# A four-layer residual stack with an RNN and an LSTM: tanh arguments in PSUM, and the LSTM's output product on GpSimd

## The chip, the cores and the metric

The kernel runs on one core of a Trainium2 chip. The metric is the device time of one execution in microseconds. The kernel before takes 3935.61 us (median of 3 runs, 3935.6 to 3937.57).

## The reference

The input x has 4 sequences of 1024 tokens of 512 numbers. Four layers follow one another, each added to its input:

```python
x = x + rnn(x)      # h = tanh(x_t @ Wx + b + h @ Wh), 1024 steps
x = x + ssm(x)      # convolution, projections, a decaying state, output projection
x = x + lstm(x)     # A = x_t @ Wx + b + h @ Wh
                    # i, f, o = sigmoid(A parts), g = tanh(A part)
                    # c = f * c + i * g ;  h = o * tanh(c), 1024 steps
x = x + x @ layer   # a layer made from the condition, once per sequence
```

The RNN and the LSTM each start from a given 4 x 512 state and are sequential: a step needs the h of the step before. The LSTM's Wh is 512 x 2048, the RNN's 512 x 512.

## The kernel before

**Chunks.** The tokens are cut into 32 chunks of 32 steps. The layers are staggered: while the RNN works on chunk i, the state-space layer works on chunk i - 1, the LSTM on chunk i - 2 and the output layer on chunk i - 3 (`chunk_work`). Each engine runs its own `body` for a chunk; the first and last chunks are written out, the others run in a loop of two chunks (`pipeline`). In a full chunk every one of the 32 steps holds one LSTM step, one RNN step and a slice of the other layers' work. There are 1024 LSTM steps; the two first chunks have RNN steps alone (64 of them).

**An LSTM step.** The state h is kept as two fp16 parts, a rounded value and the rest (`hls`), because the products with Wh, itself in two parts, are made in fp16. TensorE makes them in two halves of 256 columns (half 0 and half 1, each with its own PSUM bank `psL0`, `psL1`; 32 matmuls each, L1024 to L1046). It needs the h of half 0 first, and after 24 matmuls the h of half 1. For each half the following comes in turn; the halves are interleaved on VectorE by an order written out by hand (L866 to L890), and VectorE executes it strictly in that order:

- VectorE transposes the sums out of PSUM into `tr` (L745) and reduces them with the input part, which GpSimd had copied there (`fill`, L351), to the gates' arguments `arg` (L750).
- ScalarE makes all four gates with one tanh (`gates`, L487; sigmoid is made from tanh of half the argument), and the output gate's scaled copy `o_s` (L492).
- VectorE makes the two products i*g and f*c in one instruction (`products`, L756) and the cell (`new_cell`, L761). The cell lies beside the gates in one tile, so that one instruction can read both.
- ScalarE makes the cell's tanh (`tanh_cell`, L496).
- VectorE makes h in fp32 (`h_part`, L778, read again by the subtraction and by the next layer's input), h rounded to fp16 (`hi_part`, L781) and their difference as fp16 (`lo_part`, L785). The last one tells TensorE.

The RNN step is alike and simpler: transpose L854, reduction L859 to `arg_r`, tanh L510, the fp16 parts L898 and L900. It lies in the same queues: its transpose between the cell of half 0 and the products of half 1, its reduction ahead of `lo_part` of half 1, its fp16 parts at the end of the step, after whatever the state-space layer does on VectorE (`ssm_stage`).

**GpSimd.** In each step it copies the LSTM's input for step s + 2 into `tr`, one copy a half, each when the reduction of that half of step s is over; then the RNN's input (`fill_rnn`, L365). Every fourth step it adds the RNN's or the LSTM's outputs to the residual (L370, L377; sums of two tensors, 128 x 64).

**PSUM.** `psL0`, `psL1` and `psR` are banks of 512 fp32 columns. The matmuls of the LSTM use 256 columns of the first two, those of the RNN 128 of the third.

## Time and profile before

| | |
|---|---|
| median of 3 runs | 3935.61 us |
| lowest and highest | 3935.6 and 3937.57 us |
| span of the profiled execution | 3932.7 us |
| busy, share of the span | TensorE 92%, its weight load 78%, VectorE 83%, ScalarE 44%, GpSimd 20% |
| granted TensorE clock, mean | 0.995 of full |

The profiled execution's own total time is not among the numbers shown; what stands beside its span is the median, 2.9 us above it. The profile gives for each engine the busy time, the groups of instructions that cost most, who waited for whom, a timeline, and the chain of work that ended last. "Busy" of VectorE and ScalarE is from an instruction's start to its acknowledged end; the next one can start a little before that end, so lengths of instructions that stand one behind the other add up to more than the time they take together. Idle time is counted only from the end of the last instruction.

### The profile page before, as it was taken

The numbers are of one execution on the slowest core, as the hardware profiler recorded it, in microseconds if no ns is written. First come the engines' busy times: TensorE is split into PE (matmuls) and PEld (weight loads), VectorE is DVE, ScalarE is ACT, GpSimd is POOL, SyncE is SP. The second block draws the span as 40 slices with busy tenths as digits, with TensorE's granted clock in tenths as the row PEclk, the third lists the DMA queues.
The fourth block names the chain that finished last, engine by engine and source line by source line (L and its number), as shares of the span: only waits on it lengthen the run. The fifth ranks groups of instructions, "written<-read, shape, count | busy, mean of one in ns | idle before, by whom it ended". The sixth has DMA issues, their size and how long they took to land.

```text
span 3932.7 us, 255334 instructions
## 1 busy us (share of the span) xinstructions
PE 3630.1 (92%) x110596; PEld 3058.0 (78%) x110596; DVE 3273.3 (83%) x19155; ACT 1748.5 (44%) x8244; POOL 774.4 (20%) x3623
## 2 busy tenths in 40 slices
PE   7899999999999999999999999999999999999875
PEld 4688788888888788888888888888888888877654
DVE  6588888888888888888888888888888888888766
ACT  4244444444444444444444444444444444444432
POOL 0122222222222222222222222222222222212111
PEclk9899999999999999999999999999999999999999
DMA  7100000000000000000000000000000000000000
GB/s 275 48 7 7 10 10 10 7 7 10 10 10 9 9 7 7 10 10 10 10 7 7 10 10 10 10 7 10 7 10 10 10 10 7 7 7 7 7 6 8
DMA packets 19109, 63.32 MB, mean 16 GB/s; under 512 B 3958, under 2 KB 4526, under 8 KB 14914
## 3 DMA queue, kind: packets, MB, share of 16 engines
q1 hardware_dynamic: 17692, 46.67, 3.7%
q8 instruction: 868, 14.22, 1.5%
q14 instruction: 255, 2.09, 0.2%
q10 hardware_dynamic: 294, 0.33, 0.0%
HBM read 38.48 MB, written 8.39 MB: 12 GB/s over the span
## 4 chain that ended last, share of the span: by engine, by line
DVE 55%; PE 39%; issue 4%; ACT 1%; SPq 1%; DMA 0%; ACTq 0%; DVEq 0%; POOL 0%; POOLq 0%
PE ps_lstm L1027 32%; DVE lstm_sums L745 19%; DVE lstm_arg L750 8%; DVE lstm_ig_fc L756 7%; DVE lstm_gates_2c L761 5%; DVE rnn_sums L854 5%; DVE lstm_h_parts L785 3%; DVE lstm_h_scaled L778 2%; DVE lstm_h_parts L781 2%; PE ps_rnn L1066 2%; PE ps_lstm_in_b L1108 1%; PE ps_lstm_in_a L1171 1%; PE ps_ssm L1108 1%; SPq L301 1%; DVE rnn_h_parts L900 1%
## 5 line engine op out<-in xcount | busy, mean ns | idle before, releaser
L1027 PE MATMUL ps_lstm<-lstm_Wh_parts,lstm_h_parts 128*20 128x256 f16 x65472 | 1973.3, 273 | 259.4 <-DVE lstm_h_parts L785 246.8
L1027 PEld LDWEIGHTS ps_lstm<-lstm_Wh_parts,lstm_h_parts 128*20 128x20 f16 x65472 | 1543.1, 91 | 665.2 <-DVE lstm_h_parts L785 509.9
L487 ACT ACTIVATE lstm_gates_2c<-lstm_arg 128x32 f32<-128x32 f32 x2048 | 469.8, 229 | 1354.7 <-DVE lstm_arg L750 1354.7
L745 DVE STREAM_TRANSPOSE lstm_sums<-ps_lstm 128x256 f32<-128x256 f32 x2048 | 912.2, 445 | 191.5 <-PE ps_lstm L1027 157.4
L351 POOL COPY lstm_sums<-lstm_in 128x32 f32<-128x32 f32 x2048 | 423.7, 210 | 1749.8 <-DVE lstm_arg L750 1749.8
L1066 PE MATMUL ps_rnn<-rnn_Wh_parts,rnn_h_parts 128*20 128x128 f16 x32736 | 638.8, 220 | 22.4 <-DVE rnn_h_parts L900 20.3
L1066 PEld LDWEIGHTS ps_rnn<-rnn_Wh_parts,rnn_h_parts 128*20 128x20 f16 x32736 | 549.5, 92 | 56.2 <-DVE rnn_h_parts L900 38.5
L750 DVE TENSOR_REDUCE lstm_arg<-lstm_sums 128x32 f32<-128x96 f32 x2048 | 537.9, 263 | 35.2
L496 ACT ACTIVATE lstm_tanh_c<-lstm_gates_2c 128x8 f32<-128x8 f32 x2048 | 410.4, 200 | 253.7 <-DVE lstm_gates_2c L761 253.7
L510 ACT ACTIVATE rnn_h<-rnn_arg 128x16 f32<-128x16 f32 x1024 | 220.9, 216 | 515.8 <-DVE rnn_arg L859 515.7
L492 ACT ACTIVATE lstm_o_scaled<-lstm_gates_2c 128x8 f32<-128x8 f32 x2048 | 428.0, 209 | 33.4
L781 DVE TENSOR_TENSOR lstm_h_parts<-lstm_o_scaled,lstm_tanh_c 128x8 f16<-128x8 f32 x2048 | 332.6, 162 | 130.4 <-ACT lstm_tanh_c L496 79.1
L756 DVE SCALAR_TENSOR_TENSOR lstm_ig_fc<-lstm_gates_2c 128x16 f32<-128x16 f32 x2048 | 360.1, 176 | 15.2 <-ACT lstm_gates_2c L487 14.3
L898 DVE TENSOR_SCALAR rnn_h_parts<-rnn_h 128x16 f16<-128x16 f32 x1024 | 215.5, 210 | 176.6 <-ACT rnn_h L510 175.6
L854 DVE STREAM_TRANSPOSE rnn_sums<-ps_rnn 128x128 f32<-128x128 f32 x1024 | 315.8, 308 | 45.7 <-PE ps_rnn L1066 43.7
L785 DVE TENSOR_TENSOR lstm_h_parts<-lstm_h_scaled,lstm_h_parts 128x8 f16<-128x8 f32 x2048 | 340.4, 166 | 2.2
L778 DVE TENSOR_TENSOR lstm_h_scaled<-lstm_o_scaled,lstm_tanh_c 128x8 f32<-128x8 f32 x2048 | 334.0, 163 | 0.0
L761 DVE SCALAR_TENSOR_TENSOR lstm_gates_2c<-lstm_ig_fc 128x8 f32<-128x8 f32 x2048 | 322.0, 157 | 2.1 <-issue 2.1
L1154 PE MATMUL ps_lstm_in_b<-x,lstm_Wx 128*128 128x128 f32 x2048 | 296.5, 288 | 0.0
L1154 PE MATMUL ps_lstm_in_a<-x,lstm_Wx 128*128 128x128 f32 x2048 | 296.5, 288 | 0.0
L1154 PEld LDWEIGHTS ps_lstm_in_a<-x,lstm_Wx 128*128 128x128 f32 x2048 | 247.8, 191 | 34.1 <-issue 7.8
L1154 PEld LDWEIGHTS ps_lstm_in_b<-x,lstm_Wx 128*128 128x128 f32 x2048 | 247.8, 191 | 28.9 <-issue 1.7
(186 smaller groups left out, 2654.3 us busy)
## 6 DMA issues: line engine op xcount, KB each, us to landing
layer_plus_2I<-in_L_cond_w SPq DMA_DIRECT2D x16, 1024.0 KB, 6.3
out<-out_rows SPq DMA_DIRECT2D x128, 64.0 KB, 1.6
x_rows<-in_x SPq DMA_DIRECT2D x31, 256.0 KB
lstm_Wx<-in_L_cond_Wh SPq DMA_DIRECT2D x1, 4096.0 KB, 17.6
lstm_Wx<-in_L_cond_Wx SPq DMA_DIRECT2D x1, 4096.0 KB, 13.5
layer_plus_2I<-in_L_cond_Wh SPq DMA_DIRECT2D x1, 1024.0 KB, 9.5
rnn_Wx<-in_L_cond_Wx SPq DMA_DIRECT2D x1, 1024.0 KB, 11.7
lstm_in<-in_L_cond_w SPq DMA_DIRECT2D x1, 1024.0 KB, 10.1
```

The costliest lines, as they stand in the source:

```text
L351: Q.tensor_copy(tr[h][s % 2][:, :, XS:XS + NB], xl[par][:, s, h * HG:(h + 1) * HG, :]).then_inc(S[f"lstm_in_ready{h}"], 1)
L487: A.activation(gate[h][:, 0:G, :].rearrange("p g q -> p (g q)"), arg[h][:, :, :].rearrange("p g n -> p (g n)"), ACT.Tanh, scale=gate_scale ...
L492: A.activation(o_s[h][:, :], gate[h][:, 2, :], ACT.Copy, scale=H_SCALE, bias=H_SCALE)
L745: return mark(V.transpose(tr[h][s % 2][:, :, 0:QC], psL[h][:, 0:HW].rearrange("p (g c) -> p g c", c=QC)))
L750: V.tensor_reduce(arg[h][:, :, :], three.rearrange("p g s n -> p g n s"), AX.X, ALU.add).then_inc(S[f"lstm_summed{h}"], 1)
L756: return mark(V.scalar_tensor_tensor(out=prod[h][:, :, :], in0=gate[h][:, 0:2, :], scalar=1.0, in1=gate[h][:, G - 1:G + 1, :], op0=ALU.add ...
L761: V.scalar_tensor_tensor(out=cell[h], in0=prod[h][:, 1, :], scalar=0.5, in1=prod[h][:, 0, :], op0=ALU.mult, op1=ALU.add).then_inc(S[f"lstm ...
L785: V.tensor_tensor(half(hls, h)[:, :, LO:LO + NB], half(hl, h)[:, :, s, :], half(hls, h)[:, :, 0:NB], ALU.subtract).then_inc(S[f"lstm_h_rea ...
L854: return mark(V.transpose(tr_r[s % 2][:, :, 0:QC], psR[:, 0:RW].rearrange("p (g c) -> p g c", c=QC)))
L1027: ins = mm(psL[h][QC * j:QC * j + LO + NB, 0:HW], hls[:, k, :], whl[:, k, h, e, j, :], start=(k == 0 and e == 0), stop=(k == KB - 1 and e ...
L1066: last = mm(psR[QC * j:QC * j + LO + NB, 0:RW], hrs[:, k, :], whr[:, k, e, j, :], start=(k == 0 and e == 0), stop=(k == KB - 1 and e == 1) ...
L1154: last = mm(psI[b % 2][:, TOK * b:TOK * (b + 1)], w_, x2[:, k, :, :].rearrange("p t n -> p (t n)"), start=(k == 0), stop=(k == KB - 1))
```

## The change

The gates' arguments (`arg`, `arg_r`) are no longer tiles in SBUF but columns of PSUM banks that the matmuls leave free: both halves' in `psL0` from column 256, the RNN's in `psR` from column 128. VectorE's reductions write there, ScalarE's tanh reads there. The new cell is written to PSUM too (`cell_p`: half 0 in `psL1`, half 1 in `psR`), where ScalarE reads it for the cell's tanh; as the next step's products need it beside the gates, a new function `keep_cell` computes it a second time into the old place in SBUF, at the end of the LSTM part of the step. The fp32 h is made by GpSimd (`h_full`), for both halves after its input copies and ahead of the RNN's copy; VectorE's `h_part` is gone, and `lo_part` waits for GpSimd's semaphore as well. The waits for GpSimd's input copies move from the middle of the step to its end, and a wait for the last kept cell is added at the end of a chunk.

```diff
--- before.py
+++ after.py
@@ -167,9 +167,7 @@
         hrs = sb("rnn_h_parts", [P, KB, LO + NB], F16)
         hls = sb("lstm_h_parts", [P, KB, LO + NB], F16)
         tr_r = [sb(f"rnn_sums_{e}", [P, KB, XS + NB]) for e in range(2)]
-        arg_r = sb("rnn_arg", [P, KB, NB])
         tr = [[sb(f"lstm_sums_{h}{e}", [P, HG, XS + NB]) for e in range(2)] for h in range(NH)]
-        arg = [sb(f"lstm_arg{h}", [P, HG, NB]) for h in range(NH)]
         gate = [sb(f"lstm_gates_2c{h}", [P, G + 1, HB * NB]) for h in range(NH)]
         cell = [t[:, G, :] for t in gate]
         prod = [sb(f"lstm_ig_fc{h}", [P, 2, HB * NB]) for h in range(NH)]
@@ -203,7 +201,10 @@
         psL0, psL1, psR, psOut, psX, psS, psA, psB = [pb(n) for n in
             ("ps_lstm0", "ps_lstm1", "ps_rnn", "ps_out", "ps_x", "ps_ssm", "ps_lstm_in_a", "ps_lstm_in_b")]
         psL = (psL0, psL1)
+        arg_r = psR[:, RW:RW + KB * NB].rearrange("p (g n) -> p g n", n=NB)
+        arg = [psL0[:, HW + h * HG * NB:HW + (h + 1) * HG * NB].rearrange("p (g n) -> p g n", n=NB) for h in range(NH)]
         psI = (psA, psB)
+        cell_p = [psL1[:, HW:HW + HB * NB], psR[:, RW + KB * NB:RW + KB * NB + HB * NB]]
 
 
         d_rnnw, d_rnnx, d_x0, d_rows, d_crow, d_lstmw, d_w1, d_wx, d_ssm, d_xab, d_base, d_b2 = [sem(n) for n in
@@ -222,7 +223,7 @@
         go = {e: sem(f"go_{e}") for e in ("pe", "act", "vec", "pool")}
 
         names = [f"{n}{h}" for h in range(NH) for n in ("lstm_mm", "lstm_summed", "lstm_gated", "lstm_cell", "lstm_tanhc",
-                                                        "lstm_h_ready", "lstm_in_ready")]
+                                                        "lstm_h_ready", "lstm_in_ready", "lstm_h_full")]
         names += ["rnn_mm", "rnn_x_filled", "rnn_summed", "rnn_tanh", "rnn_h_ready", "vec_done", "pool_done", "act_done",
                   "xT_mm", "xT_ready", "l0_mm", "l0_ready", "b_mm", "c_mm", "exp_ready", "ct_ready", "y_ready", "wo_mm",
                   "x2_ready", "l2_mm", "l2_ready", "out_mm", "out_ready", "out_stored", "x1_ready", "x3_ready", "next_x_arrived"]
@@ -351,6 +352,12 @@
                         Q.tensor_copy(tr[h][s % 2][:, :, XS:XS + NB],
                                       xl[par][:, s, h * HG:(h + 1) * HG, :]).then_inc(S[f"lstm_in_ready{h}"], 1)
 
+                def h_full(h, s):
+
+                    pool.wait_ge(S[f"lstm_tanhc{h}"], s + 1)
+                    o3, t3 = [t[h][:, :].rearrange("p (b n) -> p b n", b=HB) for t in (o_s, tc)]
+                    Q.tensor_tensor(hl[:, h * HB:(h + 1) * HB, s, :], o3, t3, ALU.mult).then_inc(S[f"lstm_h_full{h}"], 1)
+
                 def fill_rnn(s):
 
                     if s >= 2:
@@ -392,6 +399,9 @@
                 for s in range(CT):
                     if w["lstm"] and s + 2 < CT:
                         fill(s + 2)
+                    if w["lstm"]:
+                        h_full(0, s)
+                        h_full(1, s)
                     if w["rnn"] and s + 2 < CT:
                         fill_rnn(s + 2)
                     if s == ARRIVE_STEP:
@@ -484,7 +494,7 @@
 
                 def gates(h, s):
                     act.wait_ge(S[f"lstm_summed{h}"], s + 1)
-                    A.activation(gate[h][:, 0:G, :].rearrange("p g q -> p (g q)"), arg[h][:, :, :].rearrange("p g n -> p (g n)"),
+                    A.activation(gate[h][:, 0:G, :].rearrange("p g q -> p (g q)"), psL0[:, HW + h * HG * NB:HW + (h + 1) * HG * NB],
                                  ACT.Tanh, scale=gate_scale).then_inc(S[f"lstm_gated{h}"], 1)
 
                 def out_gate(h, s):
@@ -493,7 +503,7 @@
 
                 def tanh_cell(h, s):
                     act.wait_ge(S[f"lstm_cell{h}"], s + 1)
-                    A.activation(tc[h][:, :], cell[h], ACT.Tanh, scale=0.5).then_inc(S[f"lstm_tanhc{h}"], 1)
+                    A.activation(tc[h][:, :], cell_p[h], ACT.Tanh, scale=0.5).then_inc(S[f"lstm_tanhc{h}"], 1)
 
                 for s in range(CT):
                     if w["lstm"]:
@@ -507,7 +517,7 @@
                         act.wait_ge(S_last["x1_ready"], len(PIECES))
                     if w["rnn"]:
                         act.wait_ge(S["rnn_summed"], s + 1)
-                        A.activation(hr[:, :, s, :], arg_r[:, :, :], ACT.Tanh, scale=rnn_scale).then_inc(S["rnn_tanh"], 1)
+                        A.activation(hr[:, :, s, :], arg_r, ACT.Tanh, scale=rnn_scale).then_inc(S["rnn_tanh"], 1)
                     if s == ARRIVE_STEP:
                         act.sem_inc(arrive, 1)
                     if known == 0:
@@ -747,7 +757,7 @@
                 def reduce(h, s, at):
                     vec.wait_ge(S["vec_done"], at)
                     three = tr[h][s % 2][:, :, :].rearrange("p g (s n) -> p g s n", n=NB)[:, :, 0:XS // NB + 1:LO // NB, :]
-                    V.tensor_reduce(arg[h][:, :, :], three.rearrange("p g s n -> p g n s"), AX.X, ALU.add
+                    V.tensor_reduce(arg[h], three.rearrange("p g s n -> p g n s"), AX.X, ALU.add
                                     ).then_inc(S[f"lstm_summed{h}"], 1)
 
                 def products(h, s):
@@ -758,8 +768,12 @@
 
                 def new_cell(h, at):
                     vec.wait_ge(S["vec_done"], at)
-                    V.scalar_tensor_tensor(out=cell[h], in0=prod[h][:, 1, :], scalar=0.5, in1=prod[h][:, 0, :],
+                    V.scalar_tensor_tensor(out=cell_p[h], in0=prod[h][:, 1, :], scalar=0.5, in1=prod[h][:, 0, :],
                                            op0=ALU.mult, op1=ALU.add).then_inc(S[f"lstm_cell{h}"], 1)
+
+                def keep_cell(h):
+                    return mark(V.scalar_tensor_tensor(out=cell[h], in0=prod[h][:, 1, :], scalar=0.5, in1=prod[h][:, 0, :],
+                                                       op0=ALU.mult, op1=ALU.add))
 
 
                 def next_x_filled(h, s):
@@ -774,14 +788,12 @@
                 o3 = [t[:, :].rearrange("p (b n) -> p b n", b=HB) for t in o_s]
                 t3 = [t[:, :].rearrange("p (b n) -> p b n", b=HB) for t in tc]
 
-                def h_part(h, s):
-                    return mark(V.tensor_tensor(half(hl, h)[:, :, s, :], o3[h], t3[h], ALU.mult))
-
                 def hi_part(h):
                     return mark(V.tensor_tensor(half(hls, h)[:, :, 0:NB], o3[h], t3[h], ALU.mult))
 
                 def lo_part(h, s, at):
                     vec.wait_ge(S["vec_done"], at)
+                    vec.wait_ge(S[f"lstm_h_full{h}"], s + 1)
                     V.tensor_tensor(half(hls, h)[:, :, LO:LO + NB], half(hl, h)[:, :, s, :], half(hls, h)[:, :, 0:NB], ALU.subtract
                                     ).then_inc(S[f"lstm_h_ready{h}"], 1)
 
@@ -856,7 +868,7 @@
                 def reduce_rnn(s, at):
                     vec.wait_ge(S["vec_done"], at)
                     three = tr_r[s % 2][:, :, :].rearrange("p g (s n) -> p g s n", n=NB)[:, :, 0:XS // NB + 1:LO // NB, :]
-                    V.tensor_reduce(arg_r[:, :, :], three.rearrange("p g s n -> p g n s"), AX.X, ALU.add).then_inc(S["rnn_summed"], 1)
+                    V.tensor_reduce(arg_r, three.rearrange("p g s n -> p g n s"), AX.X, ALU.add).then_inc(S["rnn_summed"], 1)
 
                 for s in range(CT):
                     if s == ARRIVE_STEP:
@@ -874,20 +886,20 @@
                             r_at = transpose_rnn(s)
                         p_at = products(1, s)
                         tanh_done(0, s)
-                        h_part(0, s)
-                        next_x_filled(0, s)
                         at = hi_part(0)
                         new_cell(1, p_at)
                         lo_part(0, s, at)
                         if w["mid"]:
                             ssm_stage(s, 0)
                         tanh_done(1, s)
-                        hi_part(1)
-                        next_x_filled(1, s)
-                        at = h_part(1, s)
+                        at = hi_part(1)
                         if w["rnn"]:
                             reduce_rnn(s, r_at)
                         lo_part(1, s, at)
+                        next_x_filled(0, s)
+                        keep_cell(0)
+                        next_x_filled(1, s)
+                        kept_at = keep_cell(1)
                     elif w["rnn"]:
                         r_at = transpose_rnn(s)
                         reduce_rnn(s, r_at)
@@ -901,6 +913,8 @@
                                                op0=ALU.mult, op1=ALU.subtract).then_inc(S["rnn_h_ready"], 1)
                     if known in (0, 1):
                         prepare(CT * known + s)
+                if w["lstm"]:
+                    vec.wait_ge(S["vec_done"], kept_at)
                 next_chunk(vec, "vec")
 
             pipeline(vec, body)
```

## Rows read from the trace of the kernel before

**Rows 1.** The page: span, TensorE's busy time, chain that ended last by engine.

```profile
span 3932.7 us, 255334 instructions
...
PE 3630.1 (92%) x110596; PEld 3058.0 (78%) x110596; DVE 3273.3 (83%) x19155; ACT 1748.5 (44%) x8244; POOL 774.4 (20%) x3623
...
DVE 55%; PE 39%; issue 4%; ACT 1%; SPq 1%; DMA 0%; ACTq 0%; DVEq 0%; POOL 0%; POOLq 0%
```

**Rows 2.** Timeline of one step: start us, length us, engine, line, operation, out<-in, count, [idle before].

```profile
2002.78 0.45 DVE L745 STREAM_TRANSPOSE lstm_sums<-ps_lstm 128x256 f32<-128x256 f32 x1
...
2003.27 0.26 DVE L750 TENSOR_REDUCE lstm_arg<-lstm_sums 128x32 f32<-128x96 f32 x1
2003.45 0.44 DVE L745 STREAM_TRANSPOSE lstm_sums<-ps_lstm 128x256 f32<-128x256 f32 x1
2003.57 0.23 ACT L487 ACTIVATE lstm_gates_2c<-lstm_arg 128x32 f32<-128x32 f32 x1 [1.05 <-DVE lstm_arg L750]
2003.60 0.21 POOL L351 COPY lstm_sums<-lstm_in 128x32 f32<-128x32 f32 x1 [1.14 <-DVE lstm_arg L750]
...
2003.83 0.17 DVE L756 SCALAR_TENSOR_TENSOR lstm_ig_fc<-lstm_gates_2c 128x16 f32<-128x16 f32 x1
2003.92 0.26 DVE L750 TENSOR_REDUCE lstm_arg<-lstm_sums 128x32 f32<-128x96 f32 x1
2004.10 0.16 DVE L761 SCALAR_TENSOR_TENSOR lstm_gates_2c<-lstm_ig_fc 128x8 f32<-128x8 f32 x1
...
2004.22 0.23 ACT L487 ACTIVATE lstm_gates_2c<-lstm_arg 128x32 f32<-128x32 f32 x1 [0.18 <-DVE lstm_arg L750]
...
2004.35 0.19 ACT L496 ACTIVATE lstm_tanh_c<-lstm_gates_2c 128x8 f32<-128x8 f32 x1
2004.48 0.17 DVE L756 SCALAR_TENSOR_TENSOR lstm_ig_fc<-lstm_gates_2c 128x16 f32<-128x16 f32 x1
...
2004.58 0.17 DVE L778 TENSOR_TENSOR lstm_h_scaled<-lstm_o_scaled,lstm_tanh_c 128x8 f32<-128x8 f32 x1
2004.66 0.16 DVE L781 TENSOR_TENSOR lstm_h_parts<-lstm_o_scaled,lstm_tanh_c 128x8 f16<-128x8 f32 x1
...
2004.86 0.17 DVE L785 TENSOR_TENSOR lstm_h_parts<-lstm_h_scaled,lstm_h_parts 128x8 f16<-128x8 f32 x1
...
2005.08 1.93 PE L1027 MATMUL ps_lstm<-lstm_Wh_parts,lstm_h_parts 128*20 128x256 f16 x64 [0.16 <-DVE lstm_h_parts L785]
...
2005.45 0.17 DVE L785 TENSOR_TENSOR lstm_h_parts<-lstm_h_scaled,lstm_h_parts 128x8 f16<-128x8 f32 x1
...
2006.40 0.45 DVE L745 STREAM_TRANSPOSE lstm_sums<-ps_lstm 128x256 f32<-128x256 f32 x1 [0.20 <-PE ps_lstm L1027]
```

**Rows 3.** Groups by line and shape, ScalarE: busy us, mean ns, idle before.

```profile
L579 ACT ACTIVATE out_rows<-ps_out 128x512 f32<-128x512 f32 x32 | 18.6, 580 | 4.7 <-PE ps_out L1082 4.7
...
L565 ACT ACTIVATE x_scaled<-x 128x512 f32<-128x512 f32 x16 | 9.8, 616 | 0.0
```

**Rows 4.** Groups by line and shape, VectorE: the fills of the set-up.

```profile
L601 DVE MEMSET ps_lstm<- 128x512 f32 x2 | 1.0, 485 | 0.2
...
L601 DVE MEMSET x1T<- 128x560 f32 x1 | 0.5, 525 | 0.1
```

**Rows 5.** Groups by line and shape, GpSimd: copies and a sum.

```profile
L351 POOL COPY lstm_sums<-lstm_in 128x32 f32<-128x32 f32 x2048 | 423.7, 210 | 1749.8 <-DVE lstm_arg L750 1749.8
L365 POOL COPY rnn_sums<-rnn_in 128x16 f32<-128x16 f32 x512 | 101.3, 198 | 680.9 <-DVE rnn_arg L859 674.7 <-ACT rnn_in L450 6.2
...
L377 POOL TENSOR_TENSOR x_scaled<-x_scaled,lstm_h_scaled 128x64 f32<-128x64 f32 x128 | 40.8, 319 | 1.3 <-DVE lstm_h_parts L785 1.3
```

**Rows 6.** Timeline of one step in the last chunks: GpSimd's sum beside VectorE.

```profile
3711.83 0.32 POOL L377 TENSOR_TENSOR x_scaled<-x_scaled,lstm_h_scaled 128x64 f32<-128x64 f32 x1
3711.90 0.28 DVE L756 SCALAR_TENSOR_TENSOR lstm_ig_fc<-lstm_gates_2c 128x16 f32<-128x16 f32 x1 [0.22 <-ACT lstm_gates_2c L487]
```

**Rows 7.** The page, costliest groups: the RNN's fp16 part on VectorE.

```profile
L898 DVE TENSOR_SCALAR rnn_h_parts<-rnn_h 128x16 f16<-128x16 f32 x1024 | 215.5, 210 | 176.6 <-ACT rnn_h L510 175.6
```

## The prediction

> **What bounds the kernel now.** The page comes first [rows 1]. TensorE is busy 92% of a 3932.7 us span, VectorE 83%, yet the chain that ended last is 55% VectorE and 39% TensorE: the two take turns, neither is simply full. The 1024 LSTM steps are the kernel, so one step has to be read in the timeline [rows 2]. Take the first transpose, at 2002.78, as zero. The step is then, in us: reduction of half 0 at 0.49 to 0.75, gate tanh (ScalarE) 0.79 to 1.02, products 1.05, reduction of half 1 at 1.14 to 1.40, cell 0 at 1.32 to 1.48, gate tanh of half 1 at 1.44 to 1.67, cell tanh 0 at 1.57 to 1.76, products of half 1 at 1.70, h 0 at 1.80, its fp16 part 1.88 to 2.04, its rest 2.08 to 2.25, TensorE starts at 2.30 and the next transpose at 3.62. 1024 x 3.62 = 3707 us, 94% of the span; the rest is the RNN-only head, the set-up and the tail. TensorE had been idle 0.16 before 2.30, waiting for the rest of h 0: the loop is closed by that chain, and what it gains before 2.30 moves the next step, until TensorE has no idle time left.
>
> Three readings of the same rows give the rules for the sum. A consumer starts 0.03 to 0.04 after its producer's end on VectorE and ScalarE, 0.06 on GpSimd (0.75 to 0.82), 0.05 on TensorE. VectorE starts its next ready instruction about 0.08 before the previous one's end (h 0 lasts 0.17, the fp16 part follows 0.08 later), ScalarE about 0.10 before it (1.44 + 0.23 against 1.57). And the cell tanh of half 0 did not wait for its cell (1.48 + 0.03 = 1.51) but for ScalarE, at 1.57.
>
> **The change, part by part.** *ScalarE reads PSUM instead of SBUF (gate tanh, cell tanh, RNN tanh).* The nearest pair is two Copy activations over 512 columns with immediate scale: 616 ns from SBUF, 580 ns from PSUM [rows 3]. I take 0.036 off each activation and off the time until ScalarE takes the next one. Bounds: nothing saved, and 0.05 (a third more than the pair shows, since the pair also differs in its scale and bias operands).
>
> *VectorE writes PSUM instead of SBUF (two reductions, RNN reduction, cell).* The trace has no such write with an input. It has fills: 485 ns for 512 columns in PSUM, 525 ns for 560 in SBUF [rows 4], which is 0.95 and 0.94 ns a column. I take nothing extra; a gain is not excluded by these rows, but I give it no weight, and the upper bound is what ScalarE saves, 0.036, as if the cost only moved to the writer. This is the place where a rule speaks against the change. The Trainium skill (Perfetto Trace Analysis, Optimizing Scalar/DVE Operations) puts VectorE's access overhead at about 60 ns on SBUF and 125 on PSUM, and ScalarE's at 93 and 51; by it each reduction would cost 0.065 more, the rest of h 0 would start 0.005 later than now and the kernel would stand at about 3941 us. The fills do not show such a difference, so the sum goes by them; the case is a rival below.
>
> *h moves to GpSimd.* Per half, one VectorE product of 8 columns goes (0.08 of the queue) and one GpSimd product of 128x8 comes. GpSimd's copies take 210 ns for 32 columns and 198 for 16, so about 185 ns stand without any column; its sum of two tensors of 64 columns takes 319, so 2.1 ns a column, and 8 columns give 0.20 [rows 5]. Bounds: 0.19, and the whole 0.32. What it is queued behind: the two input copies of the same step, the second starting when the reduction of half 1 ends (now 1.40) and done 0.27 later, just as the cell tanh comes; the RNN copy is put behind it and has until the next step. GpSimd is 20% busy [rows 1]. Who waits for it: the subtraction for half 0, on the chain, and behind that on VectorE everything of half 1.
>
> *The sum for half 0.* Gate tanh 0.79 to 0.98; products at 1.01 by that, but VectorE is free only at 0.67 + 0.44 - 0.08 = 1.03, so 1.03 (now 1.05). Reduction of half 1 at 1.12 to 1.38, cell 0 at 1.30 to 1.46, gate tanh of half 1 at 1.42 to 1.61. Cell tanh: 1.49 by its cell, 1.42 + 0.094 = 1.51 by ScalarE, so 1.51 to 1.67 (now 1.76). Products of half 1 at 1.64, fp16 part behind them at 1.74 to 1.90. GpSimd starts at 1.67 + 0.06 = 1.73 and ends at 1.93. The subtraction starts at max(1.90, 1.93) + 0.03 = 1.96, where it now starts at 2.08: 0.11 to 0.12 earlier.
>
> *Contention.* GpSimd's product and the fp16 part start together, and both read two SBUF tensors. When GpSimd's 64-column sum had started 0.07 ahead of a VectorE instruction with two inputs, that one took 0.28 instead of 0.17 and ended 0.35 after GpSimd's start [rows 6]. With 56 columns less (0.12) it would end 0.23 after it: the fp16 part ends at 1.96 and the subtraction starts at 1.99. The Trainium skill (SBUF — State Buffer, Who interferes with whom) says that a VectorE instruction with two SBUF inputs contends with a GpSimd one that reads SBUF; the trace agrees, 0.28 against 0.17. I take 1.98, so 0.10 a step.
>
> *Half 1* must reach TensorE after 24 of the 64 matmuls, which take 1.93 less the last one's tail: I take 0.60 after its start. Now its rest ends at 2.84, plus 0.05, against 2.30 + 0.60 = 2.90. After: cell 1 at 1.82 to 1.98, its tanh 2.01 to 2.18, GpSimd 2.24 to 2.44, subtraction 2.47 to 2.64, at TensorE 2.69, against 2.20 + 0.60 = 2.80. Covered; without that cover each 0.01 of lateness would be 0.01 a step.
>
> *The kept cell.* Two VectorE instructions of 8 columns (0.16 in the queue) come behind the subtraction of half 1, as many as the h products that go. They stand where VectorE now waits for the RNN's tanh, 176.6 us over 1024 steps, 0.17 each [rows 7]; and all of that tail moves up by 0.2 (from 2.67 to 2.47). Cover gone, they cost 0.16 a step only if VectorE reached the next transpose late; its tail is ahead of TensorE. The added waits for GpSimd's input copies are past by then. The wait at the end of a chunk is for an instruction long done. No DMA moves, so SP's queue is untouched.
>
> *What is late next.* TensorE: 0.16 idle by its matmuls less 0.10 leaves 0.06, so the gain still fits. 1024 x 0.10 = 102 us. In the 64 RNN-only steps the tanh from PSUM gives at most 0.036 each, 2 us, mostly under TensorE; I count none. The profiled execution's span is 3932.7, the median of the runs 3935.6, so 2.9 us lie around it. Its span becomes 3830, the time 3833.
>
> **The rivals.** *1. PSUM gives nothing* (VectorE pays the 0.036 that ScalarE saves). Cell tanh 0 then is 1.564 to 1.72, GpSimd 1.78 to 1.98, subtraction 2.02: 0.055 a step, 56 us, 3880. For it: no row has such a write. Against it: the fills.
>
> *2. Slower: VectorE's write to PSUM costs more than it brings.* Two reductions stand one behind the other on the chain, so each ns more counts twice, less the 0.02 of the first that VectorE's own queue hides: the subtraction starts at 1.95 + 2w (1.95: the sum without the rounding and contention). It decides from w = 0.062 on (2.07, now's start). At w = 0.09 it is 2.13, 0.055 a step later, 3992. The page rule above is w = 0.065. Against it: 485 against 525 ns in the fills.
>
> *3. GpSimd is late:* a fixed cost of two inputs that copies do not show, 0.32 for 8 columns. 1.67 + 0.06 + 0.32 + 0.03 = 2.08: no gain on the chain, 3936; with contention on top 0.02 a step slower, 3956. For it: the only two-input GpSimd instruction in the rows takes 0.32. Against it: it has eight times the columns.
>
> *4. The change does not do what it says:* VectorE's instruction count stays the same, and if TensorE were the bound the rest would vanish. The chance is small, since TensorE idles 0.16 in the step shown and waits for exactly this chain.
>
> **How the numbers follow.** Forecast (3813 to 3874) 0.62; rival 1 0.15; rival 2 0.12; rival 3 0.08, about even between no change and slower; rival 4 0.03. The forecast's own range: with 0.05 saved per activation GpSimd starts at 1.70 and the fp16 part ends at 1.93, which gives 0.12 a step, 3813; GpSimd at 0.26, half way between 0.20 and 0.32, gives 2.02 for the subtraction, 0.06 a step, 3874. The range for 8 in 10 goes from 3812 to 3950: it takes in rival 1 and most of rival 3, and leaves out rival 2's upper part. About 0.2%, 8 us, is what a measurement of this kernel can tell from no change. Faster by more than that: 0.62 + 0.15 + a part of rivals 2 and 3 = 0.80; within it 0.06; slower 0.14.
>
> **What the changed profile would show.** The step is 3.52 from transpose to transpose. Gate tanh at 0.19 (now 0.23), cell tanh of half 0 at 0.15 to 0.16 (now 0.19), reductions still 0.26. GpSimd's product of 8 columns at 0.20, starting 0.06 behind the cell tanh. The subtraction of half 0 waits for GpSimd, not for the fp16 part; TensorE's wait for it shrinks from 0.16 to 0.06. It would be wrong if the reductions came out at over 0.32, if GpSimd's product took over 0.3, if the kept cells pushed the next transpose, or if half 1 became what TensorE waits for.

## The result, and the profile after

The changed kernel takes 3971.0 us (median of 4 runs, 3967.3 to 3973.4) against 3935.6 us; the ratio is 1.0097, 95% interval 1.0082 to 1.0111. (The kernel before ran a fourth time, in 3925.1 us, and the ratio takes that run in.) It is 1% slower where 2.6% faster was forecast, and outside the range.

The page of the changed kernel, the lines that answer to [rows 1] and the groups that the change touches (columns: line, engine, operation, out<-in, count, busy us, mean ns, idle before and its releaser):

```profile
span 3970.7 us, 259462 instructions
...
PE 3638.8 (92%) x110596; PEld 3080.1 (78%) x110596; DVE 3350.7 (84%) x19155; ACT 1616.2 (41%) x8244; POOL 1216.0 (31%) x5671
...
DVE 60%; PE 32%; issue 6%; DMA 1%; ACT 1%; DVEq 0%; ACTq 0%; POOL 0%; SPq 0%; another core or an unknown queue 0%; POOLq 0%
...
L497 ACT ACTIVATE lstm_gates_2c<-ps_lstm 128x32 f32<-128x32 f32 x2048 | 403.9, 197 | 1610.9 <-DVE ps_lstm L760 1610.9
...
L359 POOL TENSOR_TENSOR lstm_h_scaled<-lstm_o_scaled,lstm_tanh_c 128x8 f32<-128x8 f32 x2048 | 419.3, 205 | 632.3 <-ACT lstm_tanh_c L506 518.1
...
L760 DVE TENSOR_REDUCE ps_lstm<-lstm_sums 128x32 f32<-128x96 f32 x2048 | 554.8, 271 | 35.2
...
L797 DVE TENSOR_TENSOR lstm_h_parts<-lstm_h_scaled,lstm_h_parts 128x8 f16<-128x8 f32 x2048 | 343.0, 167 | 104.3 <-POOL lstm_h_scaled L359 14.0
```

TensorE's busy time is about what it was (3638.8 us, 3630.1 before), VectorE's share of the chain has gone from 55% to 60%. The gate tanh is 32 ns shorter (197, 229 before), near the 36 of the forecast. The reductions are 8 ns longer (263 before). GpSimd's product takes 205 ns, as forecast. None of this says "slower", so the step has to be read as in [rows 2]. The timeline of one common step of the changed kernel:

```profile
1666.34 0.45 DVE L755 STREAM_TRANSPOSE lstm_sums<-ps_lstm 128x256 f32<-128x256 f32 x1 [0.24 <-PE ps_lstm L1041]
...
1667.00 0.44 DVE L755 STREAM_TRANSPOSE lstm_sums<-ps_lstm 128x256 f32<-128x256 f32 x1
1667.12 0.20 ACT L497 ACTIVATE lstm_gates_2c<-ps_lstm 128x32 f32<-128x32 f32 x1 [1.28 <-DVE ps_lstm L760]
...
1667.37 0.17 DVE L766 SCALAR_TENSOR_TENSOR lstm_ig_fc<-lstm_gates_2c 128x16 f32<-128x16 f32 x1
1667.47 0.27 DVE L760 TENSOR_REDUCE ps_lstm<-lstm_sums 128x32 f32<-128x96 f32 x1
...
1667.78 0.20 ACT L497 ACTIVATE lstm_gates_2c<-ps_lstm 128x32 f32<-128x32 f32 x1 [0.22 <-DVE ps_lstm L760]
...
1667.88 0.17 ACT L506 ACTIVATE lstm_tanh_c<-ps_lstm 128x8 f32<-128x8 f32 x1
...
1668.01 0.18 DVE L766 SCALAR_TENSOR_TENSOR lstm_ig_fc<-lstm_gates_2c 128x16 f32<-128x16 f32 x1
1668.10 0.16 DVE L792 TENSOR_TENSOR lstm_h_parts<-lstm_o_scaled,lstm_tanh_c 128x8 f16<-128x8 f32 x1
1668.13 0.20 POOL L359 TENSOR_TENSOR lstm_h_scaled<-lstm_o_scaled,lstm_tanh_c 128x8 f32<-128x8 f32 x1
1668.22 0.18 DVE L771 SCALAR_TENSOR_TENSOR ps_rnn<-lstm_ig_fc 128x8 f32<-128x8 f32 x1
...
1668.43 0.17 DVE L797 TENSOR_TENSOR lstm_h_parts<-lstm_h_scaled,lstm_h_parts 128x8 f16<-128x8 f32 x1
...
1668.66 1.71 PE L1041 MATMUL ps_lstm<-lstm_Wh_parts,lstm_h_parts 128*20 128x256 f16 x56 [0.18 <-DVE lstm_h_parts L797]
...
1668.99 0.17 DVE L797 TENSOR_TENSOR lstm_h_parts<-lstm_h_scaled,lstm_h_parts 128x8 f16<-128x8 f32 x1
...
1669.07 0.24 DVE L775 SCALAR_TENSOR_TENSOR lstm_gates_2c<-lstm_ig_fc 128x8 f32<-128x8 f32 x2
1669.24 0.16 DVE L910 TENSOR_SCALAR rnn_h_parts<-rnn_h 128x16 f16<-128x16 f32 x1
...
1669.98 0.45 DVE L755 STREAM_TRANSPOSE lstm_sums<-ps_lstm 128x256 f32<-128x256 f32 x1 [0.37 <-PE ps_lstm L1041]
```

(The matmul row ends where the window does.) With the first transpose, 1666.34, as zero: the cell tanh of half 0 runs from 1.54 to 1.71, where it ended at 1.76 before. Up to there 0.05 are gained. GpSimd starts its product at 1.79, 0.08 behind, and ends it at 1.99. The subtraction starts at 2.09, 0.10 after GpSimd's end; in between VectorE works only on the cell of half 1 (L771), which is over at 2.06. Before it started at 2.08. TensorE's idle time ahead of its matmuls goes from 0.16 to 0.18, and the step from 3.62 to 3.64. So GpSimd's way, from the end of the cell tanh to the subtraction, takes 0.38 where VectorE's took 0.32 (all in us), and eats more than PSUM gives.

The rest of the loss stands in single steps of a chunk. By the starts of the half 0 transposes, medians over the chunks, the common step goes from 3.618 to 3.642, but step 4 from 3.62 to 3.76, step 5 from 3.62 to 3.71, step 7 from 3.62 to 3.71, and step 8 from 3.75 to 4.06 (in every second chunk it takes 4.25). The steps of a chunk are counted from 0. These are steps in which VectorE also works for the state-space layer. By the sum of all steps the traces differ by 39 us: 26 are the common step, 14 the other steps, most of it step 8. VectorE's timeline at the end of a step 8 of the changed kernel, with GpSimd's sum of 64 columns beside it:

```profile
1632.14 0.17 DVE L797 TENSOR_TENSOR lstm_h_parts<-lstm_h_scaled,lstm_h_parts 128x8 f16<-128x8 f32 x1
...
1632.23 0.24 DVE L775 SCALAR_TENSOR_TENSOR lstm_gates_2c<-lstm_ig_fc 128x8 f32<-128x8 f32 x2
1632.33 0.32 POOL L377 TENSOR_TENSOR x1T<-xT,rnn_h 128x64 f32<-128x64 f32 x1
1632.39 0.29 DVE L840 COPY state<-stage 128x2 f32<-128x2 f32 x1
1632.60 0.59 DVE L845 SCALAR_TENSOR_TENSOR stage<-stage,softplus_A_dt 64x64 f32<-64x64 f32 x2
1633.22 0.17 DVE L910 TENSOR_SCALAR rnn_h_parts<-rnn_h 128x16 f16<-128x16 f32 x1
1633.43 0.18 DVE L912 SCALAR_TENSOR_TENSOR rnn_h_parts<-rnn_h,rnn_h_parts 128x16 f16<-128x16 f32 x1
1633.52 0.44 DVE L755 STREAM_TRANSPOSE lstm_sums<-ps_lstm 128x256 f32<-128x256 f32 x1
```

VectorE is never idle for more than 0.04 here: the two kept cells (L775), the state-space work (L840, L845), the RNN's parts (L910, L912) and at once the next transpose, which carries no idle time ahead of it. The semaphore of TensorE's half 0 had been set 0.45 before the transpose; it is late because of VectorE's queue. The same stretch of the kernel before:

```profile
1270.27 0.17 DVE L785 TENSOR_TENSOR lstm_h_parts<-lstm_h_scaled,lstm_h_parts 128x8 f16<-128x8 f32 x1
1270.35 0.16 DVE L828 COPY state<-stage 128x2 f32<-128x2 f32 x1
...
1270.42 0.59 DVE L833 SCALAR_TENSOR_TENSOR stage<-stage,softplus_A_dt 64x64 f32<-64x64 f32 x2
...
1270.57 0.32 POOL L370 TENSOR_TENSOR x1T<-stage,rnn_h 128x64 f32<-128x64 f32 x1
1271.04 0.18 DVE L898 TENSOR_SCALAR rnn_h_parts<-rnn_h 128x16 f16<-128x16 f32 x1
```

From the start of half 1's subtraction to the first of the two state-space products (L833, L845) it takes 0.15 there and 0.46 in the changed kernel. The kept cells are 0.17 of the difference. Most of the rest is the copy of the state, which takes 0.29 where it took 0.16: in the changed kernel it starts 0.06 after GpSimd's sum, in the kernel before it is over when that sum starts.

### The profile page after: what moved, and what is told of

It reads as the page before. It is cut to its first block, busy times and chain, and to the rows that moved or that the text cites. A ratio compares the mean times of both kernels' runs of the same rounds, so it can differ in the third digit from the quotient of the medians.

```text
span 3970.7 us, 259462 instructions
## 1 busy us (share of the span) xinstructions
PE 3638.8 (92%) x110596; PEld 3080.1 (78%) x110596; DVE 3350.7 (84%) x19155; ACT 1616.2 (41%) x8244; POOL 1216.0 (31%) x5671
## 4 chain that ended last, share of the span: by engine, by line
DVE 60%; PE 32%; issue 6%; DMA 1%; ACT 1%; DVEq 0%; ACTq 0%; POOL 0%; SPq 0%; another core or an unknown queue 0%; POOLq 0%
PE ps_lstm L1041 29%; DVE lstm_sums L755 20%; DVE ps_lstm L760 9%; DVE lstm_ig_fc L766 6%; DVE rnn_sums L866 5%; DVE lstm_h_parts L797 5%; DVE ps_lstm L771 4%; DVE ps_rnn L771 3%; DVE lstm_h_parts L792 2%; PE ps_rnn L1080 1%; DVE rnn_h_parts L912 1%; PE ps_lstm_in_b L1122 1%; DMA layer_plus_2I<-in_L_cond_w 1%; DVE stage L852 1%; DVE lstm_gates_2c L775 1%
## 5 line engine op out<-in xcount | busy, mean ns | idle before, releaser
L1041 PEld LDWEIGHTS ps_lstm<-lstm_Wh_parts,lstm_h_parts 128*20 128x20 f16 x65472 | 1569.1, 91 | 673.7 <-DVE lstm_h_parts L797 552.5
L497 ACT ACTIVATE lstm_gates_2c<-ps_lstm 128x32 f32<-128x32 f32 x2048 | 403.9, 197 | 1610.9 <-DVE ps_lstm L760 1610.9
L359 POOL TENSOR_TENSOR lstm_h_scaled<-lstm_o_scaled,lstm_tanh_c 128x8 f32<-128x8 f32 x2048 | 419.3, 205 | 632.3 <-ACT lstm_tanh_c L506 518.1
L760 DVE TENSOR_REDUCE ps_lstm<-lstm_sums 128x32 f32<-128x96 f32 x2048 | 554.8, 271 | 35.2
L520 ACT ACTIVATE rnn_h<-ps_rnn 128x16 f32<-128x16 f32 x1024 | 187.6, 183 | 461.5 <-DVE ps_rnn L871 461.4
L766 DVE SCALAR_TENSOR_TENSOR lstm_ig_fc<-lstm_gates_2c 128x16 f32<-128x16 f32 x2048 | 348.8, 170 | 12.1 <-ACT lstm_gates_2c L497 12.1
L506 ACT ACTIVATE lstm_tanh_c<-ps_rnn 128x8 f32<-128x8 f32 x1024 | 181.3, 177 | 220.5 <-DVE ps_rnn L771 220.5
L775 DVE SCALAR_TENSOR_TENSOR lstm_gates_2c<-lstm_ig_fc 128x8 f32<-128x8 f32 x2048 | 247.7, 160 | 1.3 <-issue 1.3
L910 DVE TENSOR_SCALAR rnn_h_parts<-rnn_h 128x16 f16<-128x16 f32 x1024 | 213.1, 208 | 17.5 <-ACT rnn_h L520 16.1
```

The costliest lines, as they stand in the source:

```text
L359: Q.tensor_tensor(hl[:, h * HB:(h + 1) * HB, s, :], o3, t3, ALU.mult).then_inc(S[f"lstm_h_full{h}"], 1)
L760: V.tensor_reduce(arg[h], three.rearrange("p g s n -> p g n s"), AX.X, ALU.add).then_inc(S[f"lstm_summed{h}"], 1)
L766: return mark(V.scalar_tensor_tensor(out=prod[h][:, :, :], in0=gate[h][:, 0:2, :], scalar=1.0, in1=gate[h][:, G - 1:G + 1, :], op0=ALU.add ...
L1041: ins = mm(psL[h][QC * j:QC * j + LO + NB, 0:HW], hls[:, k, :], whl[:, k, h, e, j, :], start=(k == 0 and e == 0), stop=(k == KB - 1 and e ...
```

## The experiments

Two theories were left after the result. A: the way to GpSimd and back costs more than PSUM brings, and the kept cells push the steps with state-space work. B: it is the writes to PSUM. "Common step" is the median step of a chunk outside the steps 1 to 9 and 31, in us; "the subtraction" is that of half 0, timed from the start of the step's first transpose. Each ratio is against runs of the kernel before on the same chip, whose medians were 3932.6 to 3935.5 us.

**1. h back on VectorE** (3912.8 us; ratio 0.9947, 0.9930 to 0.9964).

```diff
-                    if w["lstm"]:
-                        h_full(0, s)
-                        h_full(1, s)
...
                         tanh_done(0, s)
+                        h_part(0, s)
                         at = hi_part(0)
...
-                        at = hi_part(1)
+                        hi_part(1)
+                        at = h_part(1, s)
```

> The changed kernel with the fp32 h of both halves back on VectorE (h_part in its old places, no GpSimd product, no wait for it); the PSUM columns and the kept cells stay. Theory A (the handoff to GpSimd and back is what costs: 0.08 to start, 0.205 to run, 0.10 until VectorE goes on): the subtraction of half 0 starts at 2.04 to 2.05 after the first transpose instead of 2.096, a common step is 3.59 instead of 3.64, the time about 3910, below the kernel before. Theory B (VectorE's writes to PSUM and ScalarE's use of them cost more than they bring): the time stays above 3936, common step 3.62 or more.

Measured: common step 3.583, subtraction at 2.039. These are theory A's numbers, and B falls. PSUM with its kept cells is worth 0.5%; GpSimd's part takes it all and more. Step 8 is still long, 4.00.

**2. GpSimd's product alone** (4017.6 us; ratio 1.0215, 1.0198 to 1.0232): the kernel before with `h_full` and its wait, arguments and cell in SBUF.

```diff
+                    if w["lstm"]:
+                        h_full(0, s)
+                        h_full(1, s)
...
-                        h_part(0, s)
...
-                        at = h_part(1, s)
```

> The kernel before with only the fp32 h moved to GpSimd: arguments and cell stay in SBUF, no kept cells. Theory A: the subtraction of half 0 starts at 1.763 + 0.08 + 0.205 + 0.10 = 2.15 instead of 2.07, a common step is 3.69 instead of 3.62, the time about 4010, the slowest of the four. Theory B: about as fast as before or faster, 3936 or less, since no PSUM is in it.

Measured: common step 3.694. The timeline of that step, GpSimd's product and the subtraction behind it:

```profile
1686.27 0.19 ACT L505 ACTIVATE lstm_tanh_c<-lstm_gates_2c 128x8 f32<-128x8 f32 x1
...
1686.54 0.20 POOL L358 TENSOR_TENSOR lstm_h_scaled<-lstm_o_scaled,lstm_tanh_c 128x8 f32<-128x8 f32 x1 [0.17 <-ACT lstm_tanh_c L505]
...
1686.84 0.17 DVE L792 TENSOR_TENSOR lstm_h_parts<-lstm_h_scaled,lstm_h_parts 128x8 f16<-128x8 f32 x1
```

0.08 to start (1686.46 to 1686.54), 0.20 to run, 0.10 to the subtraction: the same three as with PSUM.

**3. The kept cells in idle time** (3961.6 us; ratio 1.0072, 1.0055 to 1.0089).

```diff
                         new_cell(1, p_at)
+                        keep_cell(0)
                         lo_part(0, s, at)
+                        keep_cell(1)
...
                         lo_part(1, s, at)
-                        next_x_filled(0, s)
-                        keep_cell(0)
-                        next_x_filled(1, s)
-                        kept_at = keep_cell(1)
```

> The changed kernel with the two kept cells moved into VectorE's idle time: half 0's before the subtraction of half 0, half 1's right behind it. Theory A with its second part (the kept cells at the end of the step push the state-space work and the RNN's fp16 parts in the steps 4, 5, 7 and 8 of a chunk, 0.54 us a chunk beyond the common 0.024 a step): the common step stays at 3.64, the time is about 3954. Rival (the kept cells are hidden, the steps 4 to 8 are late for another reason, for instance that VectorE's queue waits for GpSimd): no change, 3971.

Measured: common step 3.640 as in the changed kernel, steps 4, 5 and 7 back at 3.64, step 8 at 3.78; by these medians 0.54 us a chunk. (Also in the edit: the waits for GpSimd's copies stand ahead of the fp16 part of half 1, and the wait at the chunk's end is gone.) The time moves by 9 us where 17 were expected. The intervals of the two ratios just overlap (1.0055 to 1.0089 against 1.0082 to 1.0111); it is the step times that show the direction, and the size in the time is known only roughly. Moving the cells is not a cure for the common step, as A had it.

**4. Only the arguments in PSUM** (3909.6 us; ratio 0.9939, 0.9922 to 0.9955): the kernel before with `arg` and `arg_r` as PSUM columns; cell in SBUF, h on VectorE, no kept cells.

```diff
-        arg_r = sb("rnn_arg", [P, KB, NB])
+        arg_r = psR[:, RW:RW + KB * NB].rearrange("p (g n) -> p g n", n=NB)
...
-        arg = [sb(f"lstm_arg{h}", [P, HG, NB]) for h in range(NH)]
+        arg = [psL0[:, HW + h * HG * NB:HW + (h + 1) * HG * NB].rearrange("p (g n) -> p g n", n=NB) for h in range(NH)]
```

> The kernel before with only the tanh arguments (LSTM and RNN) in PSUM; cell in SBUF, h on VectorE, no kept cells. Theory A: the gate tanh of half 1 is done 0.02 to 0.03 earlier, the products and h of half 0 follow it, the subtraction starts at 2.04 to 2.05, a common step is 3.59, the head gains 3 us, the time about 3903: faster than both kernels. Theory B: 3936 or more.

Measured: common step 3.593, subtraction at 2.048. It is faster than both kernels by the smallest edit so far. The cell in PSUM on top of it (run 1) gives 0.01 a step, which does not show in the time: the kept cells come with it, and step 8 takes 3.72 here and 4.00 there.

**5. The two waits swapped** (3905.6 us, 2 runs; ratio 0.9926, 0.9908 to 0.9944). VectorE started 0.03 after its other producers; after GpSimd it took 0.10. One difference was that this instruction waits for two semaphores.

```diff
                 def lo_part(h, s, at):
-                    vec.wait_ge(S["vec_done"], at)
                     vec.wait_ge(S[f"lstm_h_full{h}"], s + 1)
+                    vec.wait_ge(S["vec_done"], at)
```

> The changed kernel with the two waits of the subtraction in the other order: first for GpSimd's product, then for VectorE's own fp16 part. In the changed kernel VectorE starts 0.101 after GpSimd's end, in both halves, where it starts 0.033 after ScalarE's end. If the 0.07 more come from the order of the two waits, the gap shrinks to 0.03 to 0.06, a common step to 3.57 to 3.60, the time to about 3900 to 3930. If the 0.10 belong to the way from GpSimd to VectorE, nothing moves: gap 0.10, common step 3.64, 3971.

Measured: the gap is 0.036, the common step 3.574. Nothing else differs, and the kernel goes from 1% slower to 0.7% faster than before. Its timeline:

```profile
1638.96 0.17 ACT L506 ACTIVATE lstm_tanh_c<-ps_lstm 128x8 f32<-128x8 f32 x1
...
1639.21 0.21 POOL L359 TENSOR_TENSOR lstm_h_scaled<-lstm_o_scaled,lstm_tanh_c 128x8 f32<-128x8 f32 x1
1639.30 0.17 DVE L771 SCALAR_TENSOR_TENSOR ps_rnn<-lstm_ig_fc 128x8 f32<-128x8 f32 x1
1639.45 0.17 DVE L797 TENSOR_TENSOR lstm_h_parts<-lstm_h_scaled,lstm_h_parts 128x8 f16<-128x8 f32 x1
```

GpSimd ends at 1639.42, the subtraction starts at 1639.45. The cell of half 1 (L771) is in the queue ahead of it as in the changed kernel and ends at 1639.47, so the 0.10 was not a wait for that cell either. The view by source line shows where the second wait went; line 796 is the wait written last in both kernels, for GpSimd in the changed one and for VectorE's own fp16 part here. First the changed kernel, then this one:

```profile
L796 DVEq EVENT_SEMAPHORE  x2048: 21/21/21, 185.7 to 3960.1; - x187
```

```profile
L796 DVEq EVENT_SEMAPHORE  x2048: 21/21/21, 182.7 to 3891.2; - x187
```

It is an instruction of its own, of VectorE's sequencer (DVEq), 2048 of them; the wait written first has none and rides on the subtraction. In the changed kernel the late semaphore is waited for by that separate instruction, and the subtraction comes behind it. The trace has times for both (medians): the separate instruction starts 0.038 after GpSimd's end, as soon as other consumers do, and the subtraction starts 0.066 after that.

**6. A spare product on GpSimd** (3920.5 us; ratio 0.9964, 0.9949 to 0.9978): run 1, and GpSimd makes the product once more into a tile that VectorE waits for only at the end of the step.

```diff
+                    Q.tensor_tensor(spare[h][:, :, :], o3, t3, ALU.mult).then_inc(S[f"lstm_h_full{h}"], 1)
...
+                        for h in range(NH):
+                            vec.wait_ge(S[f"lstm_h_full{h}"], s + 1)
                         kept_at = keep_cell(1)
```

> The variant with h on VectorE, and GpSimd makes the same product once more into a spare tile, that VectorE waits for only at the end of the step. Theory A (handoff): a common step stays at 3.58 to 3.60, since nobody on the chain waits for GpSimd, the time is about 3913 to 3920. Rival (contention: GpSimd's reads of two tensors hold up VectorE's two-input instructions on the chain): fp16 part or subtraction of half 0 start 0.04 or more later, a common step of 3.62 to 3.64, 3950 to 3970.

Measured, with h on VectorE: common step 3.595 where run 1 has 3.583; the fp16 part of half 0 takes 0.17 and the cell of half 1 starts 0.02 later. Contention is there, at 0.01 a step; it is not the loss.

**7. Only half 1's h on GpSimd** (3926.8 us; ratio 0.9985, 0.9975 to 0.9995): run 4 with `h_full(1, s)` in place of `h_part(1, s)`; the waits in the changed kernel's order.

```diff
+                        h_full(1, s)
...
-                        at = h_part(1, s)
+                        at = hi_part(1)
```

> The variant with the arguments alone in PSUM, and GpSimd makes the fp32 h of half 1 only. Theory A: the subtraction of half 0 stays at 2.05; that of half 1 starts at 2.33 + 0.08 + 0.20 + 0.10 = 2.71 to 2.72 instead of 2.65, reaches TensorE at 2.94 where TensorE, started at 2.27, wants it at 2.91: a common step of 3.61 to 3.62 instead of 3.59, about 3935. Rival (half 1 has more cover than I think): 3.59, 3910.

Measured: subtraction of half 1 at 2.72, common step 3.610 against 3.593. The cover of half 1 is as thin as its sum says: 0.07 later costs 0.017 a step. The time is 17 us above run 4's, which is what 0.017 a step gives, and 8 below the expectation.

**8. h on VectorE, kept cells behind the subtraction of half 0** (3903.3 us; ratio 0.9923, 0.9909 to 0.9936): run 1 with

```diff
                         lo_part(0, s, at)
+                        keep_cell(0)
+                        keep_cell(1)
```

and the two calls at the end of the step taken out. (Also in the edit, here and in run 9: the waits for GpSimd's copies stand ahead of the fp16 part of half 1, and the wait at the chunk's end is gone.)

> The variant with h on VectorE, arguments and cell in PSUM, with both kept cells moved behind the subtraction of half 0, into VectorE's 0.2 of idle time before the cell's tanh of half 1. Theory A with the kept cells as the cost of the steps 3 to 8: common step 3.58 as with the cells at the end, the steps 3, 6, 7 and 8 near 3.6, 3.6, 3.6 and 3.7, the time about 3900: the fastest so far. Rival (the state-space work is late anyway): 3911 to 3913.

Measured: common step 3.583; steps 7 and 8 go from 3.64 and 4.00 in run 1 to 3.61 and 3.80, but step 4 rises from 3.58 to 3.67. It has the lowest median of all; its interval overlaps those of the runs 1, 4 and 5.

**9. The changed kernel, waits swapped and kept cells there** (3909.3 us; ratio 0.9931, 0.9917 to 0.9944): run 5 with the edit of run 8.

```diff
-                        keep_cell(0)
-                        next_x_filled(1, s)
-                        kept_at = keep_cell(1)
```

> The changed kernel with the waits swapped and both kept cells behind the subtraction of half 0, in VectorE's idle time before the cell's tanh of half 1. The common step stays at 3.575, the steps 2, 3, 6, 7 and 8 lose most of their 0.35 us a chunk over the common one: about 3895, against 3906 with the waits alone swapped and 3903 with h on VectorE and the kept cells in the gap. Rival (the kept cells there hold up half 1 as much as they held up the end of the step): 3903 to 3906.

A miss: 3895 was expected, and it is no faster than run 5. The common step is 3.575, but step 8 takes 3.99, and step 31 takes 3.80 where run 5 has 3.65. The end of a step 8 in the timeline:

```profile
1606.79 0.17 DVE L797 TENSOR_TENSOR lstm_h_parts<-lstm_h_scaled,lstm_h_parts 128x8 f16<-128x8 f32 x1
...
1606.89 0.20 DVE L840 COPY state<-stage 128x2 f32<-128x2 f32 x1
...
1607.01 0.73 DVE L845 SCALAR_TENSOR_TENSOR stage<-stage,softplus_A_dt 64x64 f32<-64x64 f32 x2
1607.03 0.32 POOL L377 TENSOR_TENSOR x1T<-xT,rnn_h 128x64 f32<-128x64 f32 x1
```

The two instructions of L845 span 0.73 where they spanned 0.59 in the changed kernel, and GpSimd's 64-column sum starts 0.02 behind the first. That they meet is shown, and the other traces bear it out (medians of step 8). Where the first of the two starts 0.10 to 0.15 ahead of GpSimd's sum, it takes 0.27 and the step 3.72 to 3.80: the kernel before and the runs 3, 4 and 8. Where the two start within 0.03 of each other, it takes 0.40 to 0.43 and the step 3.90 to 4.03: the runs 1, 6, 7, 9, 10 and 11, and every second chunk of run 2. So a few hundredths of a us decide about some 0.15 there. The runs 2, 7, 10 and 11 have neither a kept cell nor the cell in PSUM, so step 8 can be long without them. No run moved GpSimd's sum alone. (In the changed kernel and the runs 5, 10 and 11 every second chunk has a step 8 that is 0.2 to 0.3 longer still, from a delay ahead of this stretch; its cause was not looked for.)

**10. GpSimd alone, waits swapped** (3956.3 us; ratio 1.0045, 1.0030 to 1.0060): run 2 with the order of run 5.

```diff
-                    vec.wait_ge(S["vec_done"], at)
                     vec.wait_ge(S[f"lstm_h_full{h}"], s + 1)
+                    vec.wait_ge(S["vec_done"], at)
```

> The kernel before with only the fp32 h on GpSimd, and the subtraction's waits swapped (GpSimd first, VectorE's own second). If the order of the waits costs 0.065 a step, the subtraction of half 0 starts at 1.763 + 0.08 + 0.20 + 0.036 = 2.08 and not 2.147, a common step is 3.625 instead of 3.694, the time about 3943 instead of 4018: GpSimd alone is then about even. If the order matters only together with PSUM, 4018.

Measured: subtraction at 2.079, common step 3.625, both as expected; the time is 13 us above the expectation, of which step 8 (3.98 on average, 3.74 in the kernel before) makes 7 to 8. The order is worth 61 us here, against 65 in run 5, and the way over GpSimd alone is still a loss: its product and the two handoffs take longer than VectorE's own product.

**11 and 12. A second wait in the kernel before.** No GpSimd product, no PSUM: a wait for the cell's tanh, long reached, is added in front of the subtraction's own wait (4018.5 us, 2 runs; ratio 1.0206, 1.0187 to 1.0224), or behind it (3943.2 us; ratio 1.0017, 1.0007 to 1.0027).

```diff
                 def lo_part(h, s, at):
+                    vec.wait_ge(S[f"lstm_tanhc{h}"], s + 1)
                     vec.wait_ge(S["vec_done"], at)
```

> The kernel before, with a second wait in front of the subtraction's own wait, for a semaphore that has long been reached (the cell's tanh): nothing is computed otherwise, no GpSimd, no PSUM. If the wait written last stands in an instruction of its own and its wake-up costs 0.065, the subtraction starts 0.10 instead of 0.035 after the fp16 part, a common step is 3.683 instead of 3.618, about 4000. If an order of waits costs nothing without GpSimd, 3936.

> The kernel before, with the same second wait behind the subtraction's own. The wait that stands alone is then the one long reached: no change, 3936, common step 3.618. If any second wait costs 0.065, wherever it stands, 4000.

Measured: in front, common step 3.689 and the subtraction 0.10 after the fp16 part's end; behind, 3.617 and 0.035. (The latter's time is 0.2% above the kernel before all the same. The common step has no part in it; in every second chunk step 8 takes 3.92 where it took 3.75, and the rest is left open. The former's time is 18 us above the expectation; its step 8 takes 4.03, and 4.34 in every second chunk.) The timeline with the wait in front:

```profile
1685.40 0.16 DVE L781 TENSOR_TENSOR lstm_h_parts<-lstm_o_scaled,lstm_tanh_c 128x8 f16<-128x8 f32 x1
1685.47 0.16 DVE L761 SCALAR_TENSOR_TENSOR lstm_gates_2c<-lstm_ig_fc 128x8 f32<-128x8 f32 x1
1685.66 0.17 DVE L786 TENSOR_TENSOR lstm_h_parts<-lstm_h_scaled,lstm_h_parts 128x8 f16<-128x8 f32 x1
```

The fp16 part ends at 1685.56, the subtraction starts at 1685.66; in [rows 2] these are 2004.82 and 2004.86. Both kernels have the same number of waits and the same 2048 separate instructions; only which semaphore stands alone differs. With the late one alone, the separate instruction starts 0.039 after the fp16 part's end and the subtraction 0.066 after that, as in the changed kernel. This is the mechanism by itself: a late semaphore that is waited for by an instruction of its own costs about 0.065 more than one waited for by the instruction that needs it.

## Why the prediction was wrong

The forecast had the subtraction of half 0 at 1.98; it came at 2.09 to 2.10. Term by term:

- **The step that failed: "1.93 + 0.03", VectorE going on after GpSimd.** The prediction carried the 0.03 over from VectorE's and ScalarE's producers. It took 0.10, +0.07. Of this 0.065 are the order of the two waits (runs 5, 10, 11 and 12), not GpSimd: the handoff itself takes 0.035. The prediction spoke of the added wait only as one more to be reached, not of how it is issued.
- **"GpSimd starts at 1.67 + 0.06".** The 0.06 is from a copy that follows VectorE; behind ScalarE's tanh it is 0.08. +0.02, in each run with the product.
- **"Reduction of half 1 at 1.12".** It was put behind the products; it waits for the second transpose, 0.67 + 0.44 + 0.03 = 1.14, which [rows 2] show. So what the gate tanh of half 0 saves is lost at once: +0.02.
- **ScalarE from PSUM.** The gate tanh gains 0.032, near the 0.036 taken; the cell tanh of half 0 gains 0.020 (192 to 172 ns): +0.015.
- **VectorE to PSUM.** Forecast nothing; the reductions take 8 ns more: +0.01. Rival 2 needed 62. The Trainium skill (Perfetto Trace Analysis, Optimizing Scalar/DVE Operations) puts VectorE's access overhead 65 ns higher on PSUM than on SBUF, and ScalarE's 42 ns lower. The 65 do not show in these writes, and the 42 show as 20 to 33; the measurement decides.
- **Contention.** 0.02 was counted and is not on the chain, since the subtraction waits for GpSimd anyway: -0.02. Run 6 puts it at 0.01. The Trainium skill (SBUF — State Buffer, Who interferes with whom) says that a VectorE instruction with two SBUF inputs contends with a GpSimd one that reads SBUF. The trace agrees: the cell of half 1, which falls into GpSimd's product, starts 0.12 behind the fp16 part in the changed kernel, 0.08 before.

The sum is 0.115 a step, x 1024 = 118 us. Forecast and time are 138 us apart.

- **"All of that tail moves up by 0.2", and the kept cells are covered.** The subtraction of half 1 moved from 2.67 to 2.65, as it pays GpSimd's way too, and with the kept cells behind it VectorE reached the RNN's parts late. The common step has room for that; the steps 4, 5, 7 and 8 do not. The prediction read the room in one common step and took it for all 32; that the kept cells push the next transpose is one of its own signs of being wrong. By the step times these four steps cost 0.54 us a chunk, some 17 us over 31 chunks; other steps are shorter, and by the sum of all steps 14 us stand beyond the common one. That is about what is left of the 138; run 3 gives back 9 of it. Not all of it is the kept cells: of the 0.31 that step 8 loses in the chunk shown, they are 0.17 and the meeting with GpSimd's sum 0.14.

What was right: that this chain closes the loop, that TensorE is not the bound, the sizes of the product and of the gate tanh, that half 1 is covered but thinly. Rival 3, GpSimd late, named the right place, at 3936 to 3956, but a product of 0.32 as its cause; the product took 0.205. That its time lies near the measured one is luck.

With the waits the other way round the change as it stands gives 0.7%. Fastest are the runs 8 (3903.3), 5 (3905.6), 9 (3909.3) and 4 (3909.6), which the intervals don't tell apart; run 4 needs the least. Left open is whether moving GpSimd's 64-column sum would give step 8 back.

## What to carry to other kernels

Where an instruction waits for two semaphores, write the one that comes last first, so that the instruction itself carries it, and look in the trace for the sequencer's separate wait instruction and its line. Take a handoff's price from a row with the same pair of engines and the same number of waits. Read the room for an instruction that is "hidden" in the fullest step of the period, not in a common one, and look there for what the other engines start at that time.

## What was not expected of the hardware

- A late semaphore waited for by a separate instruction on VectorE costs 0.10 us from the producer's end, one on the instruction itself 0.035, within VectorE as well as from GpSimd. The separate instruction itself starts on time; the 0.066 lie between it and the instruction behind it. Which wait stands apart is set by the order in which they are written: the last one.
- GpSimd starts 0.06 us after VectorE's end (copies) and 0.08 after ScalarE's (the product); which of the two differences makes it was not tried.
- VectorE's write of 32 columns to PSUM costs 8 ns more than to SBUF, ScalarE's read of them 32 ns less, and the cell tanh's read of 8 columns 20 (half 0) and 31 (half 1, 208 to 177) less.
- A 64-column sum of two tensors on GpSimd that starts within 0.03 us of VectorE's 64x64 product (runs 1, 6, 7, 9, 10 and 11) goes with 0.40 to 0.43 us for that product and not 0.27, which it takes when it starts 0.10 or more ahead of the sum.
